# Nodes' work after two attentions moved into the edge passes, with smaller edits to five other stages

## The reference

```python
x = norm(x + gcn(x))      # two convolutions: D^-1/2 (A+I) D^-1/2 (x W) + b, relu; then Wfc
x = norm(x + gat(x))      # LN, W_in; per edge e = leaky(u[src] + v[dst]); softmax over dst;
                          # sum of probs * x[src]; @ W_ff + b_ff
x = norm(x + hgt(x))      # typed k, q, v = sum_b c[type, b] * (x @ basis_b); e = q[dst] . (k att[edge_type]);
                          # softmax over dst; sum of a * v msg; typed output projection (basis a);
                          # + x @ loop_weight + bias; relu
x = norm(x + l3(x))       # h = x U^T + b; gates from V, D, E of both ends; sum over src
```

## Time and profile before

| | us |
|---|---|
| median of 3 runs (lowest, highest) | 7790.5 (7781.64, 7800.87) |
| profiled execution | 7788.46 |
| its span in the trace | 7786.7 |
| mean granted TensorE clock | 0.762 of full speed |
| busy PE / DVE / ACT / POOL | 5059.6 / 4681.0 / 3283.5 / 4933.0 |
| load, until | 38 |
| histogram | 176 |
| sort, places | 1064 |
| build | 58.2 |
| convolutions c1, c2 | 1143.8, 1079.3 |
| decode block | 14.1 |
| gat pass, n3 | 1184.4, 396.8 |
| hgt pass, n4 | 1169.4, 282.0 |
| l3 pass, n5 | 1084, 97 |

### The profile page before, as it was taken

One profiled execution on the slowest core, in us unless ns is written; L12 is line 12 of the kernel. 1 busy time (PEld: TensorE's weight loads), 2 busy tenths in 40 slices (PEclk: granted clock), 3 DMA queues, 4 the chain that ended last, 5 costly groups with the idle time before them and its releaser, 6 DMA issues. The chain is left out here.

```text
span 7786.7 us, 118192 instructions
## 1 busy us (share of the span) xinstructions
PE 5059.6 (65%) x26286; PEld 3803.4 (49%) x26287; DVE 4681.0 (60%) x12672; ACT 3283.5 (42%) x7820; POOL 4933.0 (63%) x4975
## 2 busy tenths in 40 slices
PE   6777775666665677772555557865666665777774
PEld 4555654444454555551444444435555543555553
DVE  7666664555554777774445545436666566566666
ACT  0222221444444455440444434435666541655553
POOL 0677775777776777774777770037777700777774
PEclk6666566888887888885666668977877777898897
DMA  0222221222223122233666672457777722666665
GB/s 27 59 53 54 55 55 46 54 55 55 55 55 47 53 55 54 55 52 90 179 180 179 182 164 85 143 169 221 234 225 229 216 69 80 208 201 200 201 200 139
DMA packets 818177, 921.29 MB, mean 118 GB/s; under 512 B 120930, under 2 KB 657002, under 8 KB 817706
## 3 DMA queue, kind: packets, MB, share of 16 engines
q0 software_dynamic: 198144, 441.54, 22.6%
q1 hardware_dynamic: 403498, 368.52, 15.9%
q10 hardware_dynamic: 216320, 109.07, 4.8%
HBM read 724.85 MB, written 193.87 MB: 118 GB/s over the span
## 5 line engine op out<-in xcount | busy, mean ns | idle before, releaser
L783 POOL DMA_INDIRECT arena<-t,stage_idx x3328 | 3268.1, 982 | 1249.8 <-issue 992.8
L822 PE MATMUL ps<-arena 128*128 128x128 f32 (+2 forms) x8320 | 1801.7, 378 | 770.0 <-DMA arena<-t,stage_idx 640.3
L822 PEld LDWEIGHTS ps<-arena 128*128 128x128 f32 x8320 | 1581.2, 258 | 1036.3 <-issue 935.6
L831 DVE TENSOR_TENSOR arena<-arena,ps 128x512 f32 (+2 forms) x1040 | 835.2, 803 | 733.0 <-PE ps L822 666.9
L739 POOL DMA_INDIRECT d_rec<-arena x784 | 782.5, 998 | 438.7 <-issue 241.5
L2664 POOL DMA_INDIRECT arena<-t,stage_idx x832 | 831.7, 1000 | 297.0 <-issue 224.2
L819 PE MATMUL ps<-int_tmp 128*128 128x512 bf16 (+1 forms) x1664 | 554.5, 402 | 622.9 <-DVE arena L831 340.3
L1861 PE MATMUL ps<-arena 128*128 x2496 | 393.4, 295 | 584.5 <-DVE arena L2087 323.5
L1263 PE MATMUL ps<-arena 128*128 128x416 f16 x3328 | 721.5, 368 | 0.0
L1195 ACT ACTIVATE arena<-arena 128x128 f16<-128x128 f16 x1664 | 662.2, 480 | 6.9
L1861 PEld LDWEIGHTS ps<-arena 128*128 128x128 f32 (+1 forms) x2496 | 346.6, 204 | 642.1 <-issue 620.9
(11 more groups left out here) (445 smaller groups left out, 8254.2 us busy)
## 6 DMA issues: line engine op xcount, KB each, us to landing
spill<-arena ACTq DMA_DIRECT2D x208, 512.0 KB
arena<-spill SPq DMA_DIRECT2D x208, 512.0 KB
arena<-t,stage_idx POOLq DMA_INDIRECT x4160
arena<-d_loT SPq DMA_DIRECT2D x208, 256.0 KB
arena<-s_loT SPq DMA_DIRECT2D x104, 512.0 KB, 4.8
arena<-key_d SPq DMA_DIRECT2D x98, 512.0 KB
t<-arena SPq DMA_DIRECT2D x98, 512.0 KB, 3.0
d_rec<-arena POOLq DMA_INDIRECT x784
```

Source lines behind the costliest of these rows:

```text
L783: pool.indirect_dma_start(out=rows[r][:, i, :], out_offset=None, in_=table, in_offset=bass.IndirectOffsetOnAxis(ap=stage_idx[:, 8 * r + i: ...
L822: return nc.tensor.matmul(self.banks[i // 4][:, bass.ds(self.slot[i], self.width)], weights, rows, start=False, stop=False, skip_group_che ...
L831: nc.vector.tensor_tensor(at, at, got, ALU.add).then_inc(self.added, 1)
```

## The change

It moves the nodes' work after both attentions into their passes, and edits the load, histogram, build, decode, n4 and output stages. The x tile and the edges stay on SP's queue:

```diff
-                dve.wait_ge(loads, n_all)
+                dve.wait_ge(edges_in, 16 * 12)
...
+            @block.scalar
+            def _(act):
...
+                act.dma_start(raw[5], t["L3_gnn_E_w"]).then_inc(l3_in, 16)
+                for n in w_names:
+                    act.dma_start(w[n], t[n]).then_inc(weights_in, 16)
...
+                act.wait_ge(weights_in, 16 * (len(w_names) + 2 + len(bias_names) - 1 + 1 + len(col_names)))
```

Histogram (PE), 32 products into an unused bank first and 2 after each n:

```diff
+                def zero_products(times):
+                    for _ in range(times):
+                        nc.tensor.matmul(bank(6).rearrange("p (r f) -> p r f", f=P), zeros16[:, 0:P], bcast_mid(zeros16[:, 0:P], 4), start=True, stop=True)
+                zero_products(32)
...
                         last.then_inc(free, 1)
+                        zero_products(2)
```

```diff
+        class ThirdNodes:
+            FIRST_HALF, TAIL, STEPS = 24, 2 * DONE, 5
...
+            def vector(self, dve, m, b):
+                if b == 0:
+                    self.vector_step(dve, m, [(h, t, 1) for h, t in ((4, m - 2), (2, m - 1), (0, m)) if underway(t)])
...
+            def divided(self, dve, t, w):
+                step = Chain(dve, self.a_v, 4 * t)
+                dve.wait_ge(self.sums.added, 4 * t + 24 if w == 1 else 2 * HALVES)
...
+                    if h == 3:
+                        last = nc.scalar.activation(self.dev[:, 0:w], self.arg[:, 0:w], ACT.Sqrt)
+                    else:
+                        last = nc.scalar.activation(self.aT[:, 0:D * w], self.sums_bank(w), ACT.Copy)
...
+        class FourthNodes:
+            FIRST_HALF, TAIL, STEPS = 24, 2 * DONE, 6
...
+            def scalar(self, act, m, b):
+                at = ((1, m),) if b else ((4, m - 2), (2, m - 1), (0, m))
+                self.scalar_step(act, 2 * m + b, [(h, t, 1) for h, t in at if underway(t)])
```

```diff
             def looked_up(n_b, z):
-                o_ps = n_b * 512 + z * 4 * tab_w if gat else z * 512
+                o_ps = z * 4 * tab_w if gat else 0
...
+                        looked(n, b, 0)
+                        if gat:
+                            looked(n, b, 1)
...
+                        need(pe, v_s, 2 * n - 1 if gat else 2 * n + z)
...
                             weigh(WH * lv + lj, b, 0)
+                        if not gat:
+                            looked(n, b, 1)
...
                             nc.vector.tensor_tensor(tiled(prod[:, z, :]), tiled(looked_up(b, z)), got[:, :, 0:D], ALU.mult).then_inc(v_s, 1)
-                        for z in range(2):
                             dve.wait_ge(v_s, 2 * n + z + 1)
```

n3 keeps a copy of the features (ACT), seven transposes, a copy, and the typed part; the turn's projection, norm and their transposes are gone. n4 keeps the rows part alone, with two buffers:

```diff
+        both_rows = [scratch(o, GT * R5).rearrange("p (t f) -> p t f", f=R5) for o in (TYPED_AT, AT_ACC)]
...
+                    need(dve, dma_n[k % 2], STORES * (k // 2))
...
                     for i in range(GT):
                         if i >= 2:
                             pe.wait_ge(v_r, ROWS_V * k + i - 1)
...
+                            products(x3T, W_T, 4).then_inc(w_ps, 1)
                         nc.tensor.matmul(rows_bank(i), hT[:, i * P:(i + 1) * P], VDE, start=True, stop=True).then_inc(vde_ps, 1)
-                    products(x3T, W_T, 4).then_inc(w_ps, 1)
-                    if more:
-                        loop(k + 1)
+                        if more and i == 2:
+                            transposed(k + 1)
+                        if more and i == 4:
+                            hidden(k + 1)
```

More of the change, by code:

```diff
@@ L228, in _ @@
[L228 to L243, removed]
+                    sp.dma_start(dst[:, 0:full, :], t[name][0:full * P * EC].rearrange("(j p e) -> p j e", p=P, e=EC)).then_inc(edges_in, 16)
@@ L1607, in attention_pass @@
+        def attention_pass(which, idx, table, width, keep, tab, tab_w, head_last, Nodes):
             new_stage()
@@ L2350, in _, with features @@
             def _(act):
-                def sums_T(k):
-                    act.wait_ge(t_ps, k + 1)
-                    nc.scalar.activation(aT, pair(0), ACT.Copy).then_inc(t_sb, 1)
+                def features(k):
+                    need(act, xt_ps, k)
+                    settle(nc.scalar)
+                    nc.scalar.activation(tiled(x_new), cols(x_cur, k), ACT.Copy).then_inc(x_rdy, 1)
                 def features_T(k):
@@ L2396, in rows @@
                         if more and p == 5:
-                            sums_T(k + 1)
-                        if more and p == PIECES - 2:
+                            features(k + 1)
+                        if more and p == 9:
                             features_T(k + 1)
@@ L2513, in turn @@
                     assert step.n == ROWS_V, step.n
-                ahead(dve, first, turn)
             @block.tensor
             def _(pe):
-                def add_row(name, b):
-                    for i in range(GT):
-                        last = nc.tensor.matmul(ps[:, b * 512 + i * D:b * 512 + (i + 1) * D], ones[0:1, :], bias[name][0:1, :], start=False, stop=True, skip_group_check=True)
-                    return last
-                def start(k):
-                    pe.wait_ge(a_rdy, k + 1)
-                    transposes(A, 0).then_inc(t_ps, 1)
-                    pe.wait_ge(t_sb, 2 * k + 1)
-                    pe.wait_ge(xs_in, k + 1)
-                    transposes(xs, 0).then_inc(t_ps, 1)
@@ L2567, in turn @@
+                def turn(k, more):
                     pe.wait_ge(h_sb, k + 1)
@@ L2820, in _ @@
                     one.then_inc(out_rdy, 1)
+                act.wait_ge(out_rdy, NG)
+                act.dma_start(out[(NT - 1) * P:N, :], x_cur[0:LAST, (NT - 1) * D:NT * D]).then_inc(out_rest, 16)
+                for i, number in enumerate(numbers(act, NT - 3, 2, NT - 2)):
+                    act.dma_start(out[bass.ds(P * number, P), :], x_cur[:, D * (NT - 3 + i):D * (NT - 2 + i)]).then_inc(out_rest, 16)
+                act.wait_ge(out_rest, 48)
             @block.sync
```

665 lines of the change are left out of this document (414 added, 251 removed).

## The result

The changed kernel took 7883.0 us (median; 7872.3 to 7885.9) against 7792.7 for the kernel before: a ratio of 1.0116, 95% interval 1.0103 to 1.0129. It is slower by 1.2%, outside the range of the forecast (7605 to 7745) and on the other side. The profiled execution has a span of 7883.3 us, 96.6 more than before.

A forecast was written before the change was run, and what follows sets the result against it. POOL was taken to be nearly saturated by gathers in the passes, with gaps between them to empty. The terms -13 -12 -5 -12 -31 -148 -2 +20 +84 = -119 took 7788.46 to 7669 us, range 7605 to 7745.

The forecast's parts named there:

- n4: Stage after the hgt pass: a turn falls from 37.54 to 15.5 us, 13 + 7 x 15.5 + 11 = 132, so -148 us.
- gat pass: First pass given nodes' work: 0 in rate, +16 for the last tiles, +4 for nodes' steps, +20 us in all.
- Histogram: Two added products per n raise PE's clock, PE needs 2.2 us of a pair, DVE alone bounds it: -12 us.
- rival D: Histogram: the clock stays at 0.50 and the two added products are real work, +76 us, total 7745; chance 0.07.
- hgt tail: End of the hgt pass: nodes' tail +34 and last nine halves +15, together +49 us, bounds +25 and +75.
- hgt loop: Ten hgt windows carrying nodes: 85.9 against POOL's 82.1 us, +3.8 each, taken as +35 us in all, bounds 0 and +90.
- The signs: Would show the forecast wrong: a hgt window over 90 us, a histogram longer than 176, an n4 turn over 20.
- Rival A: The hgt pass stays under POOL: 35 us less, total 7634, with shorter tails down to 7605; chance 0.2.
- Rival B: Hand-overs among ACT, DVE and PE set the hgt pass: +9 us a window, heavier tails, about 7740; chance 0.13.
- Rival E: Slower by over 0.3% if hgt's single look-up bank costs 2.2 us a half; 7874 at 3 us; chance 0.03.
- Rival C: Table loads lie on ACT's path in the hgt pass: 20 loads of 1.28 us, +26, total 7695, or 7722; chance 0.07.
- Rival F: DVE and PE still take turns in n4, a turn stays above 25 us: +66 us, total 7735; chance 0.05.

## Why the forecast failed, by its own steps

- **Load, build, decode, n3, n4, end**: right in size, to 2 us each; no run took them apart. The rows bear out the mechanism of the load (the cast waits for the edges and comes at 12.4, forecast 12.5) and of n4 (DVE and PE no longer take turns). The exact -148 of n4 has some luck in it: "a turn 15.5" was 16.3 in the mean, 5 us more over seven turns, and the two ends took some 4 less than their 24.
- **gat pass**: +27.5 for +20. From the last index copy on it is 17.5 longer (forecast 20), and the loop, for which I took 0, lost 10.
- **Histogram**: "then PE needs 2.2 us of a pair" failed; it needs 2.71. I let all of PE's work shrink with the clock; the eight small products hardly shrank (0.94 to 0.92 us), and the two zero products put PE above DVE. The clock did what rows 5 promised; rival D (clock stays) did not occur.
- **hgt tail**: +50.9 for +49, right in size; its parts were not measured.
- **hgt loop**: +230.5 for +35; this step failed. "65.9 + 12 + 8 = 85.9 against 82.1" lets DVE's work fill DVE's idle time wherever it lies, and its term "1.0 us a half" for the second look-up was a sum of durations: eight products less the reduction, and two hand-overs. It left out what is queued ahead of the look-up on PE, the weighing of the older half. Measured, DVE waits 2.6 us a half there, before any node is in the pass, which is more than all the slack I had counted (12.9 + 3.3 us a window, 2.0 a half). From then on all of DVE's 3.7 us a tile, four tiles a window, was added to the pass, where I had 3.8 us a window; the terms of the work itself were near (2.5 to 3.0 us a tile, measured 2.6 busy and 1.1 in gaps). The wait is measured; which of the two hand-overs keeps the work from being hidden was not separated.
- **The signs**: of the three named for "wrong", two came true, a hgt window of 8 x 12.65 = 101 us and a histogram of 176.4; the third, an n4 turn over 20 us, did not.
- **Rival A** fell, and with it its reason, that the second convolution carries nodes without loss. By the code that convolution has no second look-up in a bank that DVE must free first; that this makes the difference was not tested.
- **Rival B**, the rotation, has a share: 36.7 us with empty steps, and 59 to 68 back on the second kind when a step is moved. **Rival E** had the place and the direction right (the look-up of z = 1 in the single bank, with the older half's products in the same queue), but not who waits: in the 600 us PE stands there for DVE 18.1 us, DVE for PE 101.0. Its break-even of 2.2 us over the 80 halves with nodes was passed at 230.5 / 80 = 2.9. It got 0.03, because "DVE has 16 us a window of waits to absorb it"; the change itself had spent those.
- **Rival C** fell: no microsecond for the table loads, on the second kind, where it was tested. **Rival F** fell too: no n4 turn is above 18.2 us.

## What to carry to other kernels

Slack is not a number of an engine but a place in its queue. Before work is put under an engine's idle time, ask which wait ends that idle time after the change, and what is queued ahead of the releaser on its own engine. Halving a buffer between two engines, here the look-up's two banks, can turn a wait for an outside event, which absorbs work, into a hand-over inside the loop, which does not: with one bank alone DVE's waits went from 93.3 us for rows and 23.6 for look-ups to 2.7 and 148.0, and the loop grew by only 20.7 us, so that the loss shows only when work is added.

And when a clock is to rise, sort the instructions first into those that stream many columns and those that load weights for few: here only the former got shorter.

## What the runs showed that was not expected

- Full clock left products of 49 columns as long as they were: 0.92 us for eight, 0.94 at half clock, beside 0.33 for 0.51 us with 392 columns.
- Of the same program some chips took 9705 to 9710 us and others 7787 to 7793. Stages without gathers or scatters were the same to 0.3 us (n3 365.4 and 365.5), stages with them an eighth to a third longer, with PE put down to issue at every few products. The ratio of the changed kernel to the one before was 1.003 there (one run) and 1.012 on the first chip; a change's sign in such a kernel may depend on the chip.
- Twenty-one table loads of 1.28 us less in a pass gave nothing, on an engine that was 46% busy (second kind).
